# Cross-attention with two key sets on one core: the order of VectorE's outputs and of ScalarE's fifth exponentials

## What is computed

```python
q = split_heads(x @ w_q)
k, v       = split_heads(text @ w_k),  split_heads(text @ w_v)
k_ip, v_ip = split_heads(ip @ w_k_ip), split_heads(ip @ w_v_ip)
out = merge(softmax(q k^T / sqrt(32)) v)
out = out + merge(softmax(q k_ip^T / sqrt(32) + mask_ip) v_ip)
return out @ w_out + b_out + x
```

## Time and profile before

| what | us |
|---|---|
| median of 3 runs | 898.87 |
| lowest, highest of them | 893.77, 902.19 |
| the profiled execution, its own time | 901.54 |
| its span, first to last instruction | 899.7 |
| mean granted clock of TensorE | 0.954 |

### The profile page before, as it was taken

One profiled execution on the slowest core, in us unless ns is written; L12 is line 12 of the kernel. 1 busy time (PEld: TensorE's weight loads), 2 busy tenths in 40 slices (PEclk: granted clock), 3 DMA queues, 4 the chain that ended last, 5 costly groups with the idle time before them and its releaser, 6 DMA issues.

```text
span 899.7 us, 12952 instructions
## 1 busy us (share of the span) xinstructions
PE 815.8 (91%) x4381; PEld 667.1 (74%) x4381; DVE 695.0 (77%) x983; ACT 544.0 (60%) x928; POOL 623.7 (69%) x576
## 2 busy tenths in 40 slices
PE   9999889898998989898998989898998989799787
PEld 8899677686876868686776868686876768587565
DVE  7758676869677887869777887869778797969873
ACT  7765467475574847566674846566574756565642
POOL 0069467776776767687776777687776868687963
PEclk9999889899999989899999999899999999899989
DMA  9933874736557383745757383646757384444654
GB/s 326 356 106 100 268 219 147 241 133 190 196 176 234 101 275 110 218 161 188 221 176 232 108 274 122 216 147 193 215 176 223 100 264 149 155 150 152 206 165 169
DMA packets 104177, 169.99 MB, mean 189 GB/s; under 512 B 13104, under 2 KB 56112, under 8 KB 103984
## 3 DMA queue, kind: packets, MB, share of 16 engines
q1 hardware_dynamic: 103968, 167.86, 57.4%
q10 hardware_dynamic: 144, 1.31, 0.3%
HBM read 103.26 MB, written 65.54 MB: 188 GB/s over the span
## 4 chain that ended last, share of the span: by engine, by line
PE 61%; POOL 12%; DVE 10%; ACT 9%; issue 4%; DMA 3%; SPq 1%; DVEq 0%; ACTq 0%
PE bank L101 16%; PE bank L103 15%; PE bank L102 15%; PE bank L201 8%; POOL prob L253 5%; DVE res L985 2%; ACT pT_hi L738 2%; DVE pT_lo L969 2%; POOL pT_lo L590 2%; DVE xT_lo L118 2%; ACT qT L142 2%; POOL oT_lo L586 2%; PE bank L1193 2%; PE bank L1194 2%; POOL prob L260 1%
## 5 line engine op out<-in xcount | busy, mean ns | idle before, releaser
L101 PE MATMUL bank<-oT_hi,wo_hi 128*128 128x512 f32 x400 | 168.2, 420 | 48.1 <-DVE res L985 43.9
L586 POOL TENSOR_TENSOR oT_lo<-o_raw,oT_hi 128x512 fp32r<-128x512 f32 x80 | 103.9, 1299 | 129.0 <-ACT oT_hi L747 128.8
L253 POOL TENSOR_TENSOR prob<-prob,top 128x896 f32<-128x896 f32 (+1 forms) x160 | 179.9, 1145 | 15.3 <-DVE top L224 15.2
L260 POOL TENSOR_TENSOR prob<-prob,inv 128x896 f32<-128x896 f32 (+1 forms) x160 | 188.4, 1199 | 1.8
L103 PE MATMUL bank<-oT_hi,wo_lo 128*128 128x512 f32 x400 | 165.3, 413 | 0.0
L102 PE MATMUL bank<-oT_lo,wo_hi 128*128 128x512 f32 x400 | 164.4, 411 | 0.0
L101 PE MATMUL bank<-xT_hi,wq_hi 128*128 128x512 f32 x400 | 162.8, 407 | 0.0
L979 DVE TENSOR_TENSOR o_raw<-bank,pv_part 64x512 f32<-64x512 f32 x160 | 110.0, 688 | 63.6 <-ACT pv_part L743 60.8
L102 PE MATMUL bank<-xT_lo,wq_hi 128*128 128x512 f32 x400 | 158.6, 397 | 0.0
L103 PE MATMUL bank<-xT_hi,wq_lo 128*128 128x512 f32 x400 | 157.8, 394 | 0.0
L216 ACT ACTIVATE prob<-prob 128x1024 f32<-128x1024 f32 x80 | 84.1, 1051 | 107.1 <-POOL prob L253 106.9
(11 more groups left out here) (103 smaller groups left out, 1254.2 us busy)
## 6 DMA issues: line engine op xcount, KB each, us to landing
p_scratch<-stage SPq DMA_DIRECT2D x80, 512.0 KB, 3.0
prob<-p_scratch SPq DMA_DIRECT2D x320, 128.0 KB, 2.9
res<-in_xT SPq DMA_DIRECT2D x80, 256.0 KB, 5.1
outT<-res SPq DMA_DIRECT2D x80, 256.0 KB, 4.0
xin<-in_xT SPq DMA_DIRECT2D x75, 256.0 KB, 4.3
w_raw<-in_L_xattn_w_k SPq DMA_DIRECT2D x8, 320.0 KB, 4.8
w_raw<-in_L_xattn_w_k_ip SPq DMA_DIRECT2D x8, 320.0 KB, 5.0
w_raw<-in_L_xattn_w_v_ip SPq DMA_DIRECT2D x8, 320.0 KB, 4.3
```

What stands on the lines that cost most here:

```text
L101: nc.tensor.matmul(dst, a_hi, b_hi, start=first, stop=False)
L253: ins = nc.gpsimd.tensor_tensor(s, s, top[:, m, n, :].unsqueeze(2).broadcast_to([P, ROWS, k1 - k0]), ALU.subtract)
L260: ins = nc.gpsimd.tensor_tensor(s, s, inv[:, m, n, :].unsqueeze(2).broadcast_to([P, ROWS, k1 - k0]), ALU.mult)
L586: nc.gpsimd.tensor_tensor(oT_at(oT_lo, g, m), o_raw[:, (KD * g + m) % 2, :], oT_at(oT_hi, g, m).bitcast(F32), ALU.subtract).then_inc(oT_lo ...
```

## The change

Nothing is computed otherwise and no instruction is added or taken away; instructions move within the queues of four engines.

- VectorE: the sums of chunk 4 leave the end of the turn and come in the next turn behind the low part of x 1. Maxima of n's chunk 0 come behind x 2. Then output 3, turn 3, output 4, x 3, outputs 0, 1, 2, x 4, turn 4, adds 2 and 3, low part of p 4. The turn of n's chunk 0 and the low part of p 6 go behind adds 4 and 5.
- ScalarE: the exponentials of chunk 4 leave the end of the turn and come in the next turn behind move 1. The high parts of p 6 and 7 go behind moves 4 and 5, around the high part of o 2.
- GpSimd: the low part of p 7 goes behind that of o 2.
- SyncE: chunk 3 is written, outputs 3 and 4 of g - 1 are stored, chunk 3 is read back, chunk 4 is written, outputs 0 to 2 are stored, chunk 4 is read back.

```diff
--- before.py
+++ after.py
@@ -523,10 +523,16 @@
                     b = g // GPB
                     if g + 3 < NG:
                         load_x(g + 3)
-                    hand_over(g, (3, 4) if g > 0 else (4,))
                     if g > 0:
-                        for m in OUT_ORDER:
+                        write_out(g, 3)
+                        store(g - 1, 3)
+                        store(g - 1, 4)
+                        read_back(g, 3)
+                    write_out(g, 4)
+                    if g > 0:
+                        for m in range(3):
                             store(g - 1, m)
+                    read_back(g, 4)
                     for m in OUT_ORDER:
                         load_res(g, m)
                     if g % GPB == 0 and b < B - 1:
@@ -607,12 +613,11 @@
                     oT_part(g, 1)
                     if more:
                         normalise(pool, n, 0)
-                    pT_part(g, 7)
-                    if more:
                         add_mask(pool, n, 1)
                         add_mask(pool, n, 2)
                         sub_max(pool, n, 1)
                     oT_part(g, 2)
+                    pT_part(g, 7)
                     if more:
                         sub_max(pool, n, 2)
                         normalise(pool, n, 1)
@@ -787,6 +792,8 @@
                         if more_x:
                             split_x(x, 1)
                         move_pv(g, 1)
+                        if g > 0:
+                            exponentials(act, g, 4)
                         if more_x:
                             split_x(x, 2)
                         if more:
@@ -803,9 +810,7 @@
 
                     move_pv(g, 2)
                     move_pv(g, 3)
-                    pT_part(g, 6)
                     oT_part(g, 1)
-                    pT_part(g, 7)
                     if more:
                         copy_scores(act, n, 1)
                         copy_scores(act, n, 2)
@@ -814,7 +819,9 @@
                         move_q(act, x, 0)
                     move_pv(g, 4)
                     move_pv(g, 5)
+                    pT_part(g, 6)
                     oT_part(g, 2)
+                    pT_part(g, 7)
                     if more:
                         exponentials(act, n, 1)
 
@@ -848,7 +855,6 @@
                     if more_x:
                         move_q(act, x, 3)
                     if more:
-                        exponentials(act, n, 4)
                         pT_part(n, 3)
 
             @block.vector
@@ -1004,36 +1010,38 @@
                         x_lo_part(dve, x, 0)
                     if more_x:
                         x_lo_part(dve, x, 1)
+                    if g > 0:
+                        sums(dve, g, 4)
+                    if more_x:
                         x_lo_part(dve, x, 2)
+                    if more and g > 0:
+                        maxima(dve, n, 0)
                     if g > 0:
+                        output(g - 1, 3)
                         turn(dve, g, 3)
-                        output(g - 1, 3)
+                        output(g - 1, 4)
                     if more_x:
                         x_lo_part(dve, x, 3)
-                    if more and g > 0:
-                        maxima(dve, n, 0)
-                    turn(dve, g, 4)
-                    if more_x:
-                        x_lo_part(dve, x, 4)
-                    if g > 0:
-                        output(g - 1, 4)
-                    pT_part(g, 4)
                     if g > 0:
                         output(g - 1, 0)
                         output(g - 1, 1)
                         output(g - 1, 2)
-
+                    if more_x:
+                        x_lo_part(dve, x, 4)
+
+                    turn(dve, g, 4)
                     add_pv(g, 2)
                     add_pv(g, 3)
+                    pT_part(g, 4)
                     if more:
                         sums(dve, n, 0)
-                    pT_part(g, 6)
-                    if more:
-                        turn(dve, n, 0)
                         maxima(dve, n, 1)
 
                     add_pv(g, 4)
                     add_pv(g, 5)
+                    if more:
+                        turn(dve, n, 0)
+                    pT_part(g, 6)
                     if more:
                         maxima(dve, n, 2)
                         sums(dve, n, 1)
@@ -1056,7 +1064,6 @@
                         turn(dve, n, 2)
                         sums(dve, n, 3)
                         pT_part(n, 2)
-                        sums(dve, n, 4)
                 for m in OUT_ORDER:
                     output(NG - 1, m)
 
```

## The result

The changed kernel takes 832.18 us (829.92 to 832.81, four runs) against 897.08 for the kernel before in the same comparison: ratio 0.9267, 95% interval 0.9217 to 0.9318, so 7.3% faster. The forecast was 849 us, range 830 to 884. The sign, the mechanism of the wait and the place were right; the time lies 2 us above the lower edge of the range, among the times of rival B. The profiled execution took 832.34 us with a span of 830.5 and a clock of 0.988. In the kernel after, L991 is the output addition, L985 the value addition, L1200 and L1201 the value products, L592 and L596 GpSimd's low parts of o and of p; lines up to L471 keep their numbers.

What follows compares the result with a forecast made beforehand. TensorE was taken to bound the kernel, stalled by VectorE's queue order before output 0. Turns falling from 50.84 to 47.3 give 46 over 13 turns, plus 1 and 3: 50 off 901.5, 851.5 profiled, median 849, range 830 to 884.

Steps and rivals of the forecast that it cites:

- rival B: VectorE's outputs come in time: idle 0.1 + 0.2, no half rate, turn 44.9; 818 us, up to 835; chance 0.14.
- The queries: ScalarE moves queries ahead of the scores once chunk 4's exponentials leave the turn's end; TensorE's idle 1.0 per turn goes.
- rival D: Slower: chunk 4's chain ahead of VectorE's outputs delays them if GpSimd's subtraction ends after t = 3.05; 907 us; chance 0.05.
- VectorE's chain: VectorE's queue up to output 0: TensorE starts at 13.45, idle 1.6 in place of 3.60; bounds 0.1 and 3.1.
- Scores waiting for adds: TensorE's next scores newly wait for VectorE's adds 2 and 3: idle 0.3 a turn, bounds 0 and 1.0.
- Low part of p 7: GpSimd ends it at 28.35, TensorE wants it at 28.2: idle 0.2 a turn, bounds 0 and 1.3.
- The clock: Half rate behind TensorE's wait for output 0: 0.6 of 1.6 us a turn kept, bounds 0 and 1.6.
- The ends: Gains outside the 13 turns: 1 us in turn 14, 3 us in the last turn from the high part of o 1.
- SyncE, forecast 0: SyncE's new order reads chunk 3 back about 4 us earlier; effect on the path 0, bounds -0.2 to +0.3.
- A: The forecast itself: VectorE's chain stays the last, idle 1 to 3 a turn; 836 to 864 us; chance 0.58.
- C: One or two more VectorE meetings with GpSimd per turn, each 1.5 us; 869 and 888 us; chance 0.18.
- E: The wait for output 0 only becomes waits for adds and p part 7; 895 to 902 us; chance 0.05.

Runs made afterwards that it cites:

- the second half alone: The changed kernel with the exponentials and sums of chunk 4 back at the turn's end, against the kernel before: 835.10 us, ratio 0.9284.

## Why the forecast was right, and where its size was off

- **The wait that bounds the kernel, and why.** Right. Putting outputs 0 to 2 back behind turn 4, x 4 and p 4, and nothing else, costs 61 to 63 us.
- **The queries.** Right that the idle 1.0 a turn goes. In ScalarE's timeline the exponentials of chunk 4 start at 385.52 and 432.12, t = 3.1 in both kinds of turn, as counted (3.05), so rival D's point of decision was never reached. What the forecast didn't price by itself is that the 1.6 of sums moves into the chain ahead of the outputs: alone it pays back all it gains.
- **VectorE's chain.** TensorE goes on at t = 13.81 and 13.01, forecast 13.45. Idle 1.27 in the mean instead of 1.6. In the turn with keys x 0 is held up as told (1.92), in the other less (1.19); x 3 meets the subtraction only in the turn without keys (1.80), while in the one with keys x 2 meets the low part of o 0 (1.69) instead. So there is one meeting ahead of output 0 besides x 0, as forecast, but only in every second turn the one that was named. The Trainium skill ("SBUF — State Buffer", section "Who interferes with whom") has a Vector instruction with two SBUF inputs and a GpSimd instruction that reads SBUF exclude each other for a whole instruction. That is what the rows give: the x part begun at 439.51 lasts 1.80, near the rest of GpSimd's first part (1.71 of the 2.52 from 439.06, so 1.26) and then its own 0.63 alone, 1.89.
- **Scores waiting for adds.** Forecast idle 0.3, none shown: the adds end at t = 18.1 and 17.3, just as TensorE comes. **Low part of p 7.** GpSimd ends it at t = 28.5 in the turn with keys (28.35 forecast), and TensorE's gap there is 0.2, as forecast. Products with such small gaps take 44.9 a turn, 44.63 forecast.
- **The clock, the step that failed.** "The idle pieces are below half as long as the one that was followed by half rate, so of the 1.6 I keep 0.6." None is kept: the clock of the main loop is 1.00, also behind idle times of 1.68. This is 0.6 x 13 = 7.8 us, the largest term. The bound of 0 was stated; the value was set between the bounds, as if half rate went down with the length of the stall. It doesn't: how often it follows a stall is counted in the last section, and stalls of 1.68 are short enough to be followed seldom, not short enough to be safe. The reading that led to it was right in size (1.6 missing; the trace of before has 22.1 / 13 = 1.7), but rows 3 already show a stall of 3.60, at 428.10, with no half rate behind it, and two turns of before have 1.98 and 2.02 in place of 3.60, because half rate behind the wait for queries had made TensorE late there.
- **The sum.** Forecast 47.3 a turn, measured 46.17. With 50.89 for the mean turn of before in place of 50.84 that is 61.4 - 46 = 15.4 us more: clock 7.8, idle before L101 0.33 x 13 = 4.3, adds 0.3 x 13 = 3.9, p 7 hidden in the products' small gaps 0.2 x 13 = 2.6, less 0.27 x 13 = 3.5 for the longer products, together 15.1. The ends gave 69.2 - 61.4 = 7.8 instead of 4, because turn 0 gained too. Together 19.2: 851.5 forecast for the profiled execution, 832.3 measured. All the misses but the longer products lie on the same side, and they nearly carried the time out of the range.
- **SyncE, forecast 0.** Wrong as the price of leaving the edit out: the new order of VectorE needs it, 8 to 10 us. As the price of the edit in the old order it was not run. Moving p 6 and 7, with turn 0 and maxima 1, is worth 7 to 8 us in the same way, where the forecast had it as a small cost in the turn and 3 us in the last one. The forecast asked what each part gives beside the kernel before; the runs show a part that gives nothing alone (the exponentials) and two that cost 7 to 10 when they are missing (p 6 and 7, SyncE).
- **The rivals.** A's mechanism held: the idle before L101 is still VectorE's chain, 1.27. B's time was reached with only half of B's terms, no half rate and no wait for adds, and without its idle of 0.1. C fell: no further meeting was paid. D and E fell.

## What to carry to other kernels

When a stall is followed by half rate, price the two apart (here half rate was some 21 of the 65 us), and don't scale the half rate with the stall: count in the traces at hand which stalls are followed by it and which aren't. A move in a queue is a trade with all that it passes: one half of this change gave 0 alone and the other nearly all, and of that the small moves on SyncE and of p kept 7 to 10 us each. Before an instruction is pushed back because its result is wanted late, look for an in-order queue that has it at its head: putting turn 4 on VectorE behind two short steps cost 13 us more, by its timelines through SyncE's queue.

## What the runs showed of the hardware that was not expected

- **The same idle time with and without half rate behind it.** In the kernel before, the waits for queries of 1.78 and 1.79 were followed by the lower clock in two of seven cases; in the kernel with the second half alone, those of 1.6 to 1.8 at the same place in one of seven (336.90), and not at 430.83 (0.40 at 432.73 above). A line of before, and the case of the second half alone:

```profile
363.33 1.16 PE L201 MATMUL bank<-k_diag,qT 64*128 64x128 f32 x16 [1.79 <-ACT qT L142]
...
365.00 0.63 PE L103 MATMUL bank<-oT_hi,wo_lo 128*128 128x512 f32 x1
```

```profile
336.90 1.16 PE L201 MATMUL bank<-k_diag,qT 64*128 64x128 f32 x16 [1.78 <-ACT qT L142]
...
338.65 0.63 PE L103 MATMUL bank<-oT_hi,wo_lo 128*128 128x512 f32 x1
```

  Counted over the main loops of all fourteen kernels, half rate followed none of 82 stalls of 0.8 to 1.5, 5 of 44 from 1.5 to 1.95, both of 1.98 and 2.02, 3 of 6 from 2.3 to 3.3 and 35 of 37 of 3.5 and more. So one idle time doesn't decide it, and it is not gone for certain below half of 3.60. What else decides was not settled.
- **Products that nothing needs keep the clock up.** 12 of them in a wait, 2.88 us, gave 21 us over the kernel, with the output itself no sooner.
- **Both sides pay when they meet.** Where x 3 lasts 1.80 instead of 0.69 behind GpSimd's first part, GpSimd's second part (128 x 128) ends 0.8 after the first instead of 0.4: 2.52 for the pair at 439.06, 2.06 where nothing meets it.
